# The values times Wv·Wm ahead of the attention, in place of the merged outputs behind it

## The reference

```
q = x @ Wq.T + bq ;  k = key @ Wk.T + bk ;  v = value @ Wv.T + bv
scores = (q @ k.T) / 64 * adj ;  where |scores| < 1e-5: -1e9
h = softmax(scores) @ v @ Wm.T + bm
x1 = layernorm(x + h)
out = layernorm(x1 + relu(adj @ x1 @ W.T + b))
```

## Time and profile before

| | |
|---|---|
| median of 3 runs | 2011.98 us |
| profiled execution | 2021.37 us |
| its span on the core | 2019.6 us |
| mean granted TensorE clock | 0.989 of full |
| PE busy | 1938.3 us (96%), 8859 matmuls |
| DVE busy | 1543.1 us (76%) |
| ACT busy | 872.1 us (43%) |
| POOL busy | 165.0 us (8%) |

### The profile page before, as it was taken

One profiled execution on the slowest core, in us unless ns is written; L12 is line 12 of the kernel. 1 busy time (PEld: TensorE's weight loads), 2 busy tenths in 40 slices (PEclk: granted clock), 3 DMA queues, 4 the chain that ended last, 5 costly groups with the idle time before them and its releaser, 6 DMA issues.

```text
span 2019.6 us, 26392 instructions
## 1 busy us (share of the span) xinstructions
PE 1938.3 (96%) x8859; PEld 878.7 (44%) x8859; DVE 1543.1 (76%) x3203; ACT 872.1 (43%) x1166; POOL 165.0 (8%) x262
## 2 busy tenths in 40 slices
PE   8988999999999999998999999999999799999998
PEld 5433444444444444443444444444444344444443
DVE  7898788888888846766777777777677337788887
ACT  5775555565666554544554555555454100000000
POOL 6000000000000020000000000001001000000000
PEclk9998999999999999999999999999999999999999
DMA  8657998899999897878778778777878987555551
GB/s 296 230 175 176 236 263 220 208 257 245 259 246 261 214 314 199 206 154 157 172 177 159 183 172 178 182 176 175 165 181 204 217 254 161 125 129 137 133 134 60
DMA packets 582118, 393.21 MB, mean 195 GB/s; under 512 B 479728, under 2 KB 506352, under 8 KB 580208
## 3 DMA queue, kind: packets, MB, share of 16 engines
q1 hardware_dynamic: 550624, 269.55, 56.7%
q0 software_dynamic: 31376, 122.17, 22.2%
HBM read 190.32 MB, written 117.44 MB: 152 GB/s over the span
## 4 chain that ended last, share of the span: by engine, by line
PE 71%; DVE 9%; DMA 8%; SPq 5%; ACT 3%; issue 3%; DVEq 0%; ACTq 0%
PE ps L1081 23%; PE ps L1060 22%; PE ps L1224 16%; DMA PT<-Phl 5%; PE ps L1094 3%; PE ps L1109 3%; SPq L458 2%; DMA UT<-Uhl 2%; PE ps L1013 2%; DVE prob L1982 1%; PE ps L1179 1%; ACT prob L1433 1%; DVE Phl L2010 1%; ACT Phl L1441 1%; SPq L605 1%
## 5 line engine op out<-in xcount | busy, mean ns | idle before, releaser
L1081 PE MATMUL ps<-V,PT 128*128 128x512 f16 x3072 | 704.1, 379 | 3.8 <-issue 3.7
L1060 PE MATMUL ps<-KG,left 128*128 128x512 f16 x2688 | 626.9, 382 | 28.4 <-ACT ps L1421 17.6
L1081 PEld LDWEIGHTS ps<-V,PT 128*128 128x128 f16 x3072 | 300.4, 98 | 367.7 <-issue 6.5
L1060 PEld LDWEIGHTS ps<-KG,left 128*128 128x128 f16 x2688 | 262.4, 98 | 355.7 <-issue 46.7
L1428 ACT ACTIVATE small<-prob 128x512 f32<-128x512 f32 x256 | 159.4, 628 | 266.9 <-DVE prob L1982 244.9
L2010 DVE SCALAR_TENSOR_TENSOR Phl<-prob,Phl 128x2048 f16<-128x2048 f32 x64 | 146.7, 2292 | 114.7 <-ACT Phl L1441 81.2
L1421 ACT ACTIVATE ps<-ps 128x512 f32<-128x512 f32 x192 | 111.4, 580 | 180.0 <-PE ps L1060 180.0
L1994 DVE CUSTOM_DVE_ANT_0 prob<-prob,small 128x512 f32<-128x512 f32 x256 | 173.7, 688 | 2.9
L1988 DVE TENSOR_SCALAR small<-small,eps_s,neg_s 128x512 f32<-128x512 f32 x256 | 136.8, 543 | 35.5 <-ACT small L1428 33.6
L1670 ACT ACTIVATE p<-ps 128x512 f32<-128x512 f32 x14 | 8.4, 597 | 348.0 <-PE ps L1224 348.0
L1441 ACT ACTIVATE Phl<-prob 128x2048 f16<-128x2048 f32 x64 | 121.9, 1904 | 53.8 <-DMA PT<-Phl 51.8
(11 more groups left out here) (225 smaller groups left out, 2020.6 us busy)
## 6 DMA issues: line engine op xcount, KB each, us to landing
adjh<-in_adj POOLq DMA_DIRECT2D x64, 512.0 KB, 8.3
adj_bf<-adjh SPq DMA_DIRECT2D x32, 512.0 KB, 6.8
adj_bf<-adjh POOLq DMA_DIRECT2D x32, 512.0 KB, 7.4
left_dram<-left SPq DMA_DIRECT2D x16, 896.0 KB, 5.9
xraw<-in_x_t SPq DMA_DIRECT2D x8, 1024.0 KB, 8.8
t_dram<-tq POOLq DMA_DIRECT2D x8, 1024.0 KB, 5.5
t<-t_dram SPq DMA_DIRECT2D x32, 256.0 KB, 7.8
x_in<-in_x SPq DMA_DIRECT2D x32, 256.0 KB, 3.2
```

The source lines that it names most:

```text
L1060: last = nc.tensor.matmul(ps[:, bank, :], left[:, s, k, d * P:(d + 1) * P], KG[gr][:, RIGHT[k], m, d, :], start=(first and n == 0), stop=( ...
L1081: last = nc.tensor.matmul(ps[:, BU + b, :], PT[:, b, s, m, :], V[:, v, m, :], start=(m == 0 and n == 0), stop=(m == MT - 1 and n == 2))
```

## The change

1. The 4096 rows of values come to the kernel with each 128-row tile turned block by block (`value_t`, made by the host's layout), so that a tile of values can be the stationary operand of a matmul.
2. `values_product(m)` multiplies value tile m by `Wvm` in 12 matmuls, 32 tiles in all. ACT (`values_out_high`) and DVE (`values_out_low`) write the result's halves over the tile. Tiles 0 to 7 stand in the preparation (G = 4 to 7), 8 to 13 in period 0, 14 and 15 in period 1, and 16 to 31 in the step periods, two in each. The last ones go through bank `BX` and `vvhl`.
3. `project`, `merge`, `merged_high`, `merged_low`, `first_scaled` and the turns of the merged rows are gone. In their place DVE adds x to the scaled first output (`first_added`), and `z_made` adds the second output from weigh's bank.
4. The orders follow: in the step periods the split of the second values goes to group 0; in the second pass `z_made`, `x1_row`, `x1_low`, the turns of x1 and `rows_product` take other places, the late part of `left` is loaded at a period's start, and POOL loads adj only once the x1 rows of tile 2i − 4 are turned.

```diff
+                def values_product(m):
+                    if m < MT:
+                        pe.wait_ge(v_lo, m // TC + 1)
+                        wait(pe, vw_lo, m - 1)
+                        bank, tile = BU + m % 2, V[:, :, m, :]
+                    else:
+                        pe.wait_ge(b_lo, 2 * ((m - MT) // 2) + 2)
+                        pe.wait_ge(vw_lo, m)
+                        bank, tile = BX, vvhl[:, :, m % 2, :]
...
+                def values_out_high(m):
+                    act.wait_ge(vw_mm, m + 1)
+                    bank, into = (BU + m % 2, V[:, HI, m, :]) if m < MT else (BX, vvhl[:, HI, m % 2, :])
+                    nc.scalar.activation(into, ps[:, bank, :], ACT.Copy, scale=V_DOWN).then_inc(vw_hi, 1)
...
+                def values_out_low(m):
+                    dve.wait_ge(vw_hi, m + 1)
...
                 def period(q):
+                    second = MT + 2 * (q - FIRST_STEP) if FIRST_STEP <= q < FIRST_STEP + STEPS else None
...
                     scores(q, 0, P2)
                     if q >= 2:
                         weigh(g1 - 2, 2)
                     if i >= 2:
-                        project(2 * i - 4)
+                        rows_product(2 * i - 4)
...
                     if q >= 1:
                         weigh(g0, 0)
+                    if second is not None:
+                        values_product(second)
...
                     scores(q, 1, P2)
+                    if second is not None:
+                        values_product(second + 1)
...
                         weigh(g0, 3)
+                    if i >= 2:
+                        rows_product(2 * i - 3)
...
                     threshold(q, 0, C11)
+                    if FIRST_STEP <= q < FIRST_STEP + STEPS:
+                        second_values_low(q - FIRST_STEP)
...
                     masked(q, 1, C11)
                     if FIRST_STEP <= q < FIRST_STEP + STEPS:
-                        second_values_low(q - FIRST_STEP)
+                        values_out_low(MT + 2 * (q - FIRST_STEP))
...
+                def first_added(n):
...
+                    nc.vector.scalar_tensor_tensor(out=o_in[:, b, :], in0=o_in[:, b, :], scalar=wn[:, i % 2, b, 0:1],
+                                                   in1=x_in[:, b, :], op0=ALU.mult, op1=ALU.add).then_inc(o_sc, 1)
...
                 def z_made(n):
-                    nc.vector.scalar_tensor_tensor(out=z_out[:, b, :], in0=ps[:, BX, :], scalar=inv_vw[:, 0:1],
-                                                   in1=x_in[:, b, :], op0=ALU.mult, op1=ALU.add).then_inc(s_z, 1)
+                    nc.vector.scalar_tensor_tensor(out=z_out[:, b, :], in0=ps[:, BU + b, :], scalar=wn[:, i % 2, b, 1:2],
+                                                   in1=o_in[:, b, :], op0=ALU.mult, op1=ALU.add).then_inc(s_z, 1)
```

POOL's part of it, at the head of its `second_period`:

```diff
                     i = q - NP
+                    if i >= 2:
+                        pool.wait_ge(x1t_in, 32 * (2 * i - 3))
                     if i >= 1:
                         for b in range(2):
                             load_adj(q, b)
```

More of the change, by code:

```diff
@@ L1016, in queries @@
                     last.then_inc(t_mm, 1)
+                def values_product(m):
[7 more added lines that the diff above has]
+                        bank, tile = BX, vvhl[:, :, m % 2, :]
+                    q = 0
+                    for s, w in PASSES:
+                        for k in range(KD):
+                            last = nc.tensor.matmul(ps[:, bank, :], tile[:, s, k * P:(k + 1) * P], Wvm[:, w, k, :],
+                                                    start=(q == 0), stop=(q == 3 * KD - 1))
+                            q += 1
+                    last.then_inc(vw_mm, 1)
                 for G in range(NG):
@@ L1030, in _ @@
                         queries(G, e)
+                        if G >= TC and e % 2 == 1:
+                            values_product(2 * (G - TC) + e // 2)
                 def scores(q, gr, k):
@@ L1406, in _ @@
                         key_high(0, P4)
+                    if G >= TC:
+                        values_out_high(2 * (G - TC) + 1)
+                for k in (P1, P7, P6, P2):
+                    key_high(1, k)
                 act.wait_ge(s_sig, 2)
@@ L1512, in first_period @@
                     seed(q, 1, BU2)
+                    if FIRST_STEP <= q < FIRST_STEP + STEPS:
+                        values_out_high(second + 1)
                     if q + 1 < NP:
@@ L1887, in _ @@
                         rows_low(G + 1)
+                    if G > TC:
+                        values_out_low(2 * (G - TC) - 1)
                     if G == 0:
@@ L2282, in second_period @@
                     added(q, 0, C21)
+                    small_scores(q, 0, C11)
+                    masked(q, 0, C22)
                     if i >= 2:
-                        merge(2 * i - 3)
-                    small_scores(q, 0, C11)
+                        z_made(2 * i - 3)
+                    threshold(q, 0, C11)
                     if i >= 2:
-                        merged_low(2 * i - 3)
-                    masked(q, 0, C22)
+                        x1_row(2 * i - 3)
                     small_scores(q, 0, C22)
-                    threshold(q, 0, C11)
                     masked(q, 0, C21)
@@ L2309, in second_period @@
                     if i >= 2:
-                        z_made(2 * i - 3)
+                        y_low(2 * i - 4)
                     added(q, 1, C22)
-                    if i >= 2:
-                        x1_row(2 * i - 3)
-                    if i >= 1:
-                        merge(2 * i - 2)
                     added(q, 1, C21)
+                    masked(q, 1, C22)
                     if i == 1:
```

387 lines of the change are left out of this document (169 added, 218 removed).

## The result

The changed kernel takes 2225.2 us (median of 4 runs, 2214.2 to 2235.7) against 2009.7 us before (2007.5 to 2013.2): ratio 1.107, interval 1.1012 to 1.1127. The forecast was 2081 with a range of 2000 to 2118. The direction was right, the size was off by 144 us.

A forecast was written before the change was run, and what follows sets the result against it. PE is busiest and its work only moves, so idle time and waits where it goes decide. +19 + 85 - 7 - 28 = +69 on the median of 2012.0 gives 2081 us, range 2000 to 2118 for 8 in 10.

The forecast's parts named there:

- Part 1: Start: 192 more matmuls on PE and 3.6 us of waits, +19 us; bounds +16 and +28.
- Part 2: Step periods: 192 more matmuls plus waits for second values and bank BX, periods 49.5 against 38.85 us, +85 us.
- rival C: Waits also lower PE's clock: 2 us for each of 21 waits, +42, giving 2123 us; chance 0.15.
- Part 3: Second pass: fewer matmuls but P5 of group 1 waits, periods 48.8 us, -7 us; bounds -94 and +10.
- X: Second pass: time into a period when DVE's wait for the low PT transpose ends; taken as 19.6 us.
- the formula: Second pass: period = 44.0 + (X + 17.6 - 32.4) = X + 29.2 us, 48.8 with the X taken.
- late turns: Second pass, i = 3 to the last P3: some 24 of 26.8 us lost before are single late transposes, which stay.
- Part 4: End: 270 matmuls, waits of 3.9 and 2 us, 64.2 against 91.9, -28 us; bounds -32 and -15.
- A: Second pass: turns of PT land early, X 14.8 or less, -94 there, sum -17, 1995 us; chance 0.12.
- B: Step periods: second values are ready when PE asks, +41 there, sum +25, 2037 us; chance 0.12.
- D: Whole kernel: PE stays the bound everywhere, equal matmuls mean equal time, within 6 us of 2012; chance 0.05.

The follow-up runs named there:

- the loads early: The changed kernel, but POOL loads adj at the head of its second-pass period without waiting for the turned x1 rows: 2120.8 us, ratio 1.051.
- products later: The changed kernel with both values products of a step period behind later weighs and ACT's two high halves behind later magnitudes: 2164.5 us, ratio 1.071.
- the loads and the seeds early: The changed kernel with adj loads not waiting, values products moved later, and ACT's second-pass group 1 seeds BCU, BU2 ahead of two magnitudes: 2010.4 us, ratio 1.001.
- the seed first: The changed kernel, but on ACT seed CD of group 0 stands ahead of the second prob_high: 2229.6 us, ratio 1.107.

## Why the prediction was right and wrong

**Part 1, the start.** Right: +21.1 against +19. The four waits that I had put at 0.3, 1.6, 0.7 and 1.0 us were 0.23, 2.42, 0.40 and 1.75.

**Part 2, the step periods.** Right in mechanism and, but for one term, in size: 27.4 us in eight waits for `second_values_low` (forecast 8 x 3.7) and 8 x 1.63 for `BX`. The term that was mis-sized is the clock. I had it as rival C, apart from the sum, but the forecast's own waits of over 3 us bring it on: seven of the eight times the next twelve matmuls took 4.1 to 4.45 us and not 2.75. That is 11 of the missing 13 us.

**Part 3, the second pass.** This is the step that failed, in one term: "I take X = 19.6", with X = 21 as the bound. X was 24.7 to 29.5, 26.7 on average. What I built on it held: P5 of group 1 came at X + 17.7 in this trace, and in that of the loads early in i = 3 to 14 (forecast X + 17.6), and the period here at X + 29.2 within 2.4. With X = 26.7 the formula gives 55.9 us, 7.1 more than my 48.8, and 13 x 7.1 = 92 us, where 85 were missing. That these agree so well is in part luck, for two other terms nearly cancel: my sum has 24 us of late turns on top, which the measured X already holds, and it has no term for the lower clock behind the waits, nor the late X of the last period (30.2). Without the 24 us the formula gives 723 us for this stretch and the trace shows 740; 12 of the 17 us are periods of 56.9 and not 55.9 us. I had seen that adj's loads would start "about 7 us into it, into the turns of PT", and priced that at nothing, even taking X 0.8 us earlier than before. The first experiment takes the wait away and gets 104 us back, the second puts it into the kernel before and loses 52. With the loads early X is 18.7 and the stretch 642.3 us, so 19.6 and 654.5 were fair for a kernel whose loads had stayed where they were.

The Trainium skill, "DMA: Bandwidth & Descriptors", section "Issuing engines are not separate DMA queues", says that DMAs started by the scalar, sync or gpsimd engine run on the same 16 DMA engines and interleave. The runs agree: SP's high transpose is held for 6.8 us on average beside POOL's loads, and for 2.1 with the loads moved away. I named this rule and its sign, and left its size out of the sum.

The price stood in the trace of before, too. In nine of its twelve periods i = 3 to 14 the first load of adj goes out 0.90 to 0.92 us in, and X is 20.5 to 24.2. In the other three it goes out at 1.08, 2.02 and 3.34 us, and X is 25.1, 28.6 and 26.5, the three latest. The middle one, from 928.00, POOL's loads and SP's high transpose:

```profile
930.02 1.09 POOL L821 DMA_DIRECT2D adjh<-in_adj  x2 [1.11 <-DVE prob L1982]
...
936.35 10.70 SPq L458 DMA_TRANSPOSE PT<-Phl  x1
```

I had booked such periods as "single late turns, which stay". They were samples of the X that goes with a later load: by the formula, 13 periods with X = 28.6 take 747 us, some 85 more than the 662.6 of before, where 77 more were measured.

**Part 4, the end.** Too hopeful by 12 us. weigh of tile 62 started 20.9 us behind the last P3 (1767.75 - 1746.87), not 17; and the wait of 7.50 us for the first turned adj rows was not in the sum at all. No experiment was made on it; that the loads of y beside it are the cause is a guess, not shown. The end takes 75.8 us here and 76.2 with the loads early, so the wait ahead of adj's loads is not its cause.

**Rivals.** A would have needed X of 14.8; no kernel here reached it (16.6 at best). B did not occur in the changed kernel, but products later shows its floor to be real. C came true on top of the forecast: PE's busy time rose by 45.6 us at equal matmuls, against its price of 42. D is excluded.

## What to carry to other kernels

A wait added to a load costs where the load lands, not where it waits: look at which transfer on the path it will now run beside, and price that transfer from the samples of the trace in which the load came late. The longest wait on the busiest engine need not be worth anything (6.7 us a period at P3: nothing), if another wait hangs on the same event. And order edits are not additive: a row moved into an idle stretch gained 32 us while the transpose was late and nothing when it was early.

## What was unexpected in the hardware

- The same `PT` transpose holds SP's queue for a time that depends on what POOL moves beside it. Means for the high half: 6.1 to 6.9 us where adj's first load goes out 1.0 to 1.5 us ahead of it (6.8 with the stores beside it, 6.9 with them away), 5.0 and 4.2 where the loads go out earlier and land 3.7 to 4.6 us behind its issue, 2.1 to 2.3 where they have landed by then, to within 0.2 us. The single times in the changed kernel run from 2.1 to 8.4 us; the 2.1 is in the one period whose loads go out 1.2 us behind it. Where inside a DMA the time goes, no run shows.
- The stores act on the landing more than on the hold. With the loads and the seeds early, moving the stores away leaves the low half's hold at 3.0 us, but it lands 6.6 us behind its issue and not 8.1.
- In the traces the granted clock falls behind most waits of PE of over 3 us. In the changed kernel, between 196 and 1850 us, 29 of 30 such waits (those whose next twelve matmuls run without another wait) were followed by twelve matmuls of 4.0 to 5.3 us in place of 2.75; behind waits of 1 to 2 us it was 1 of 16, behind 2 to 3 us 2 of 6. The exception is a wait of 3.25 us, and in the kernel with the seed first all eight waits of 2 to 3 us had slow matmuls behind them, so there is no fixed price for a length of wait. From i = 3 to the last P3 the clock was 0.92, against 0.99 before.
